# Preparation of keys, weights and angles moved into the attention loop of a two-layer cross-attention and expert kernel

## The reference, cut to what matters

```python
x = x + _L0_xattn_ref(_layernorm(x), ctx_2048, Wq, Wk, Wv, Wo, q_norm_w, k_norm_w, pos_BxS2, itok)   # 16 heads, 4 key heads of 128
x = x + _L0_ffn_ref(_layernorm(x), ...)                  # 32 experts, top 6, and shared ones
x = x + _L1_xattn_ref(_layernorm(x), ctx_2048, seg_id, W_kvc, W_dq, W_uq, W_qr, W_uk, W_kr, W_uv, W_o)
x = x + _L1_ffn_ref(_layernorm(x), ...)
...
kv_in = jnp.concatenate([context_hidden, draft_hidden], axis=1)          # 1601 + 256 = 1857 rows
k = _rms_norm((kv_in @ Wk.T).reshape(bsz, total_len, KVH, HD), k_norm_w)
q = _rope(q, draft_position_ids); k = _rope(k, full_position_ids)
probs = jax.nn.softmax(jnp.einsum('bhqd,bhkd->bhqk', q, k) * SCALE, axis=-1)
...
kv_c = kv @ W_kvc                                        # third block
k_rope = _rope(kv_c @ W_kr, lk)
```

## Time and profile before

| | |
|---|---|
| median of 3 runs | 1956.87 us |
| the profiled execution, first to last instruction | 1959.5 us |
| PE, DVE, ACT, POOL busy | 88%, 74%, 55%, 56% |
| `prepare` (first DMA to the first load of `attend`) | 0.72 to 128.60 us |
| first score matmul of group 0 | 173.94 us |
| one group in the steady part | 72.8 us |

### The profile page before, as it was taken

How to read it: one execution, slowest core, us unless ns; L and a number is a source line. 1 busy time by engine, 2 the same in 40 slices (tenths; PEclk the granted TensorE clock), 3 DMA queues, 4 the chain that set the end, 5 groups by cost and what they waited for, 6 DMA issues and landing times. The chain is left out here.

```text
span 1959.5 us, 41434 instructions
## 1 busy us (share of the span) xinstructions
PE 1725.4 (88%) x14663; PEld 1326.9 (68%) x14663; DVE 1442.7 (74%) x3812; ACT 1070.1 (55%) x2650; POOL 1091.2 (56%) x1657
## 2 busy tenths in 40 slices
PE   3346999999999999999999999996899999079997
PEld 3234787787787778778778778775555555038974
DVE  7838878877877877877877887875757775675746
ACT  3324766767666667666666766763133333073543
POOL 4525866866866776776776776710156664072210
PEclk9678999999999999999999999997899999595998
DMA  7683021121021022022022020144369996510100
GB/s 283 227 323 130 2 89 46 45 88 57 34 88 69 22 89 75 16 89 88 2 89 88 2 89 13 49 147 184 109 198 272 270 269 194 163 31 16 44 10 26
DMA packets 76663, 201.96 MB, mean 103 GB/s; under 512 B 9993, under 2 KB 42866, under 8 KB 73266
## 3 DMA queue, kind: packets, MB, share of 16 engines
q1 hardware_dynamic: 63314, 163.70, 24.5%
q0 software_dynamic: 9984, 30.42, 4.6%
q10 hardware_dynamic: 3168, 5.24, 0.7%
HBM read 161.67 MB, written 37.66 MB: 102 GB/s over the span
## 5 line engine op out<-in xcount | busy, mean ns | idle before, releaser
L893 DVE TENSOR_TENSOR att_pT<-att_pT 128x512 bf16<-128x512 f32 (+1 forms) x512 | 321.2, 651 | 179.7 <-ACT att_pT L790 176.5
L643 PE MATMUL att_out<-att_V,att_pT 128*128 128x128 bf16 x5760 | 386.0, 220 | 10.0 <-DVE att_pT L893 8.3
L643 PEld LDWEIGHTS att_out<-att_V,att_pT 128*128 128x128 bf16 x5760 | 349.6, 98 | 37.5 <-DVE att_pT L893 19.7
L790 ACT ACTIVATE att_pT<-att_pT 128x512 bf16<-128x512 f32 (+1 forms) x512 | 277.9, 572 | 175.6 <-PE att_pT L631 175.6
L796 ACT ACTIVATE att_prob<-att_scores,att_negmax 128x512 f32<-128x512 f32 (+1 forms) x512 | 329.8, 654 | 21.1 <-DVE att_negmax L882 18.9
L622 PE MATMUL att_scores<-att_K,att_Q 128*128 128x512 bf16 (+1 forms) x1536 | 324.1, 361 | 1.0 <-DVE att_K L855 1.0
L880 DVE TENSOR_REDUCE att_mx<-att_scores 128x1 f32<-128x512 f32 (+1 forms) x512 | 291.4, 631 | 1.2 <-PE att_scores L622 1.2
L631 PE MATMUL att_pT<-att_ident,att_prob 128*128 128x128 f32 x1920 | 274.3, 274 | 0.0
L622 PEld LDWEIGHTS att_scores<-att_K,att_Q 128*128 128x128 bf16 x1536 | 150.6, 98 | 145.4 <-issue 2.5
L582 PE MATMUL att_aux<-att_wkv,att_kvT 128*128 128x256 bf16 x1440 | 179.6, 274 | 43.8 <-DMA att_kvT<-kv_s 20.0
L631 PEld LDWEIGHTS att_pT<-att_ident,att_prob 128*128 128x128 f32 x1920 | 208.6, 141 | 0.9
(11 more groups left out here) (312 smaller groups left out, 3233.5 us busy)
## 6 DMA issues: line engine op xcount, KB each, us to landing
moe_wa<-in_wa_l SPq DMA_DIRECT2D x80, 480.0 KB
att_kvT<-kv_s SPq DMA_DIRECT2D x15, 1920.0 KB
att_tab<-tab_s SPq DMA_DIRECT2D x16, 960.0 KB, 11.5
att_wq<-wq_s SPq DMA_DIRECT2D x16, 512.0 KB
att_wo<-wo_s SPq DMA_DIRECT2D x16, 512.0 KB
kv_s<-prep_kvhl SPq DMA_DIRECT2D x4, 1920.0 KB
prep_kv<-in_ctx_l SPq DMA_DIRECT2D x4, 1664.0 KB, 8.1
moe_y<-y_s SPq DMA_DIRECT2D x8, 768.0 KB, 4.7
```

The source lines that it names most:

```text
L643: last = nc.tensor.matmul(out_ps[:, i % 2, :], pT[:, i % 2, a, k, :], V[:, par, k, w, :], start=(k, a, w) == (0, 0, 0), stop=(k, a) == (KT ...
L790: nc.scalar.activation(pT[:, i % 2, 0, 4 * j:4 * j + m, :], pT_ps[j % 2][:, 0:m, :], ACT.Copy).then_inc(s["pt_hi"], 1)
L893: nc.vector.tensor_tensor(pT[:, i % 2, 1, 4 * j:4 * j + m, :], pT_ps[j % 2][:, 0:m, :], pT[:, i % 2, 0, 4 * j:4 * j + m, :], ALU.subtract) ...
```

## The change

`prepare` is gone, with its scope. Its work goes into `attend`:

- Batch 0 is split in SBUF at the start: ACT makes the high halves of keys and weights, POOL the low halves of the keys, DVE those of the weights, and DVE forms the angles of batch 0 only. Nothing of it passes through DRAM before it is used. The first projections begin with context keys (KV2), not with the tokens.
- Batches 1 to 3 are split a quarter of the keys at a time: in groups 0 to 11, at the end of slot 2, ACT (`keys_high`) and then DVE (`keys_low`, with a sum of the keys).
- The remaining weights come in nine pieces in groups 0 to 2, high halves on ACT in slots 1 and 4, low halves on POOL (`weight_low`) after the third and the eighth rope of its sequence.
- The angles of the next batch are nine DVE steps, one a slot, in groups 1, 5, 9 and 2, 6, 10; the two Sin instructions stand on ACT at the end of slot 6 of groups 2, 6 and 10.
- The key table is made by quarters: a `TB` task on PE in slot 3 of every group (in bfloat16 halves now), a copy by ACT, the turning by POOL (`turn_rows`) after the sixth rope. A `MN` task gives the mean from the key sums. An `XT` task turns the next batch's tokens in groups 1, 5 and 9.
- POOL gathers batch by batch, in groups 4, 8 and 12, and for the last batch at the end.
- The halves of the keys stay in SBUF for a batch; the weights are written to DRAM and loaded again from group 4 on.

Core of the diff:

```diff
 SLOTS = [
     ([], [("KV", 0)], [("KV", 1)]),
     ([("AT-", 1)], [("KV", 2)], [("WO-", 1)]),
-    ([], [("Q", 0)], [("KV", 3)]),
-    ([], [("Q", 1)], [("KV", 4)]),
+    ([("XT", 0)], [("Q", 0)], [("KV", 3)]),
+    ([("TB", 0)], [("Q", 1)], [("KV", 4)]),
...
-    ([("KT", 2)], [("KT", 3)], []),
+    ([("KT", 2)], [("KT", 3)], [("MN", 0)]),
...
+PIECES_AT = {(0, 1): [(1, "O")], (0, 4): [(2, "K"), (2, "Q")], (1, 1): [(3, "K"), (3, "Q")], (1, 4): [(2, "O")], (2, 4): [(3, "O")]}
...
+                    elif kind == "TB":
+                        b, k = divmod(n, NB)
+                        pe.wait_ge(s["wcat_lo"], 1)
+                        keys_split(pe, min(k + 2, NB), b)
+                        for m in range(min(4, CT - 4 * k)):
+                            k0 = S + (4 * k + m) * P
+                            for c in range(DC):
+                                for a, w in ((0, 0), (0, 1), (1, 0)):
...
+                    if i == 2 and g < SPLITS:
+                        keys_high(g)
+                    for h, kind in PIECES_AT.get((g, i), ()):
+                        weight_high(h, kind)
+                    if i == 6 and g % KVH == 2 and g < (B - 1) * KVH:
+                        turn_table(g // KVH + 1)
...
+                def keys_low(g):
...
+                    nc.vector.tensor_tensor(kvT[:, b % 2, 1, :, cols], keys, kvT[:, b % 2, 0, :, cols], ALU.subtract).then_inc(s["c_lo"], 1)
+                    nc.vector.reduce_sum(sums[:, b, k, :], keys, AX.X).then_inc(s["c_sum"], 1)
...
+                def between(i, g):
+                    b = g // KVH + 1
+                    if (g, i) == (0, 0):
+                        for k in range(NB):
+                            nc.vector.reduce_sum(sums[:, 0, k, :], first_part(k), AX.X).then_inc(s["first_sum"], 1)
+                        weight_low_first("O")
...
+                    if g < SPLITS:
+                        if i == 2:
+                            keys_low(g)
+                        if g % KVH == 1 and i == 0:
+                            normal_rows(b)
+                        if g % KVH == 1 and i >= 3:
+                            angle(b, i - 3)
+                        if g % KVH == 2 and 1 <= i <= 4:
+                            angle(b, i + 4)
...
+                def turn_rows(n):
...
+                    nc.gpsimd.tensor_tensor(turned[:, 0, 0:m, :], keys, turns[:, 0, 0:m, :], ALU.mult).then_inc(s["turned"], 1)
+                    nc.gpsimd.tensor_tensor(turned[:, 1, 0:m, 0:RH], keys[:, :, RH:R1], turns[:, 1, 0:m, 0:RH], ALU.mult).then_inc(s["turned"], 1)
+                    nc.gpsimd.tensor_tensor(turned[:, 1, 0:m, RH:R1], keys[:, :, 0:RH], turns[:, 1, 0:m, RH:R1], ALU.mult).then_inc(s["turned"], 1)
...
+                    nc.gpsimd.tensor_tensor(keys, turned[:, 0, 0:m, :], turned[:, 1, 0:m, :], ALU.add).then_inc(s["tb_ready"], 1)
...
                 def prep(g, par):
-                    pool.wait_ge(tab_load[par], 16 * (g // 2 + 1))
+                    pool.wait_ge(s["trig_ready"], 2 * (g // KVH) + 2)
+                    now = g - 1
                     for order, (kind, n) in enumerate(POOL_ORDER):
                         rope(pool, order, kind, n, g, par)
+                        if order == 2:
+                            for h, k in PIECES_AT.get((now, 1), ()):
+                                weight_low(h, k)
+                        if order == 5:
+                            turn_rows(now)
+                            if now == 0:
+                                rstd(slice(2, TT), 2)
+                        if order == 7:
+                            for h, k in PIECES_AT.get((now, 4), ()):
+                                weight_low(h, k)
+                        if now >= KVH and now % KVH == 0:
+                            b = now // KVH - 1
+                            if order in (2, 6):
+                                gather(2 * b + order // 6)
+                            if order in (4, 8):
+                                store(2 * b + order // 8)
```

More of the change, by code:

```diff
@@ L488, in nth, with first_key_rows @@
+        FREE = {"KV": "kvraw_ready", "Q": "qraw_ready", "KT": "kt_lo", "QT": "qt_lo", "AT": "at_lo", "WO": "x_added", "XT": "xt_lo", "TB": "tb_raw", "MN": "mean_ready"}
         def nth(kind, n, g):
+            if kind in ("XT", "TB", "MN"):
+                return n + 1
+            if kind == "KV" and g == 0:
+                return FIRST_KV.index(n) + 1
             return PER_GROUP[kind] * g + n + 1
+        def first_key_rows(eng, pairs):
+            done = [p for p in FIRST_KV if p in pairs or FIRST_KV.index(p) < max(FIRST_KV.index(q) for q in pairs)]
+            wait(eng, s["kp_vector"], sum(("KV", p) not in FIRST_ON_POOL for p in done))
+            wait(eng, s["kp_pool"], sum(("KV", p) in FIRST_ON_POOL for p in done))
@@ L496, in key_rows @@
             elif g == 0:
-                on_pool = sum(("KV", j) in FIRST_ON_POOL for j in range(n + 1))
-                wait(eng, s["kp_vector"], n + 1 - on_pool)
-                wait(eng, s["kp_pool"], on_pool)
+                first_key_rows(eng, [2 * (n // 2), n])
         def bank_of(kind, n, g):
@@ L565, in task @@
                     par = (u + ahead) % 2
+                    b = gt // KVH
                     bank = bank_of(kind, n, gt)
-                    if gt or kind not in ("KT", "QT"):
+                    if not (gt == 0 and kind in ("KT", "QT")) and (kind, n) != ("XT", 0):
                         if before:
@@ L648, in slot @@
                 def slot(i, g, u, first, prep, last):
-                    ahead, amid, behind = (tasks_of(place, prep, first, last) for place in SLOTS[i])
+                    ahead, amid, behind = (tasks_of(place, prep, first, last, g) for place in SLOTS[i])
                     old = not (first and i == 0) and not (last and i > 0)
```

827 lines of the change are left out of this document (456 added, 371 removed).

## The result

Four runs of the changed kernel have a median of 1946.72 us (1944.51 to 1948.19), four of the kernel before, on the same chip, 1957.4 us (1956.04 to 1962.97). The ratio is 0.9939, with a 95% interval of 0.9924 to 0.9954. So the kernel is faster, by 11 us where 57 were forecast, and its time lies above the range of 1880 to 1920 us and above the wider one of 1864 to 1932.

What follows compares the result with a forecast made beforehand. PE, 98% busy, was taken to bound the kernel, with POOL's chain 0.8 us from the bound; 1959.5 - 114.9 (start) + 54.0 (groups) + 1.6 (DVE, group 0) + 3 (clock) = 1903.2 profiled, 1900 us median, range 1880 to 1920, wider 1864 to 1932.

Steps and rivals of the forecast that it cites:

- the 114.9 us: Start: first scores come near 59 us instead of 173.9, giving back 114.9 us.
- the first scores at 24 + 34.9: Start: rope chain begins at 24 us and takes 34.9 as before, so first scores at 59.
- 54.0 forecast: Attention groups: added POOL work costs 54.0 us in all, paid by PE as a wait of KT3 for POOL.
- POOL's chain in a group has 0.8 us to spare, against PE's none: Steady group: POOL ends KV7's rope only 0.8 us before PE's KT3 needs it.
- after 625.26 only one wait of 2.52 us is left on the way to KV7: Steady group: POOL's one later wait, 2.52 us, takes up added work standing before it; later work lengthens the group.
- `keys_low` with its sum is 2.2 in slot 2; DVE waits 2.34 there, so nothing: Slot 2, DVE: the added 2.2 us fit into its 2.34 us wait and cost nothing.
- so I charge nothing: Slot 6, ACT: 4.3 us for Sin, three times, covered by PE's slot 7 wait for POOL; without cover 6 us.
- PE alone (1869): Rival for the groups: PE alone sets the pace, its added tasks costing 25.4 us, plus 1.6; 1869 us, chance 0.17.
- Rival 2: Groups: waits lower the clock in most groups, not three, 22 to 33 us on top; 1920 to 1935 us, chance 0.17.
- The forecast's own 3 us for the clock: Groups 0 to 2: POOL's stalls lower PE's clock, costing 3 us in all.
- Rival 3: Start: first stage not short, first scores at 80 to 90 us; kernel 1921 to 1931 us, chance 0.07.
- Rival 4: All 16 groups: POOL late through every rope; slower if each grows over 7.2 us, 2000 us with 10; chance 0.04.

Runs made afterwards that it cites:

- the experiment on the start: Changed kernel, POOL's first rope not waiting for the small product, second head's low weight halves held until DVE's last rope: 1941.65 us, ratio 0.9911.
- the placed version: Changed kernel with the start's two edits, rows behind last rope, keys rounded in slot 1, angles, Sin, deviations, mean, gathers and weights re-placed: 1894.0 us, ratio 0.9661.
- the last version: The placed version with Sin in slot 0 of groups 3, 7, 11, POOL's weight pieces re-placed, `first_rows` moved to group 3: 1878.83 us, ratio 0.9586.

## Why the prediction was wrong

**The start** was right in kind: of the 114.9 us that it was to give back, 108.05 came (173.94 to 65.89). The chain began at 25.18 (24 forecast). What failed is "the first scores at 24 + 34.9": the chain itself was 5.8 us longer than in the kernel before, and the experiment on the start returned 5.2 of them (its chain took 35.3, from 25.39 to 60.72). One part, POOL's wait for the small product, was foreseen but held in the 4 us ahead of the chain; it came inside. The other, turns taken by DVE and POOL, was charged in the angles and not in the chain's last steps, beside the second head's weights. The Trainium skill (SBUF — State Buffer, "SBUF: two separate sides") describes the port pair that these two share as an exclusive lock: a DVE instruction with two inputs in SBUF waits out the whole of a GpSimd instruction that reads SBUF and began first. By that rule DVE's step of 0.22 us ends just behind POOL's, and the trace agrees (63.24 and 63.17 us). One reading of the earlier trace rows was loose, without harm: DVE's step there ended 2.0 us after POOL's and not just after it, which is about the step's own length (2.16), so the conclusion that the two took turns stands.

**The groups** hold the large miss: 54.0 forecast and 95.1 measured. The step that failed is "POOL's chain in a group has 0.8 us to spare, against PE's none", and what was built on it: that POOL's lateness at KT3 is the whole price and all else lies beside it. KT3 waited 16.7 us for POOL in all the groups, not 54; the rest of the 95.1 was paid by PE's own added tasks and by its waits for DVE and ACT in other slots. Three readings under it were wrong.

- "after 625.26 only one wait of 2.52 us is left on the way to KV7": that wait is not spare time ahead of a fixed end. What ends it is DVE's sum in slot 3, which moves with every delay of slots 2 and 3. So the chain starts anew there, and PE's added task of 1.50 us is paid ahead of POOL's rows, not beside them. Rows 5 of the kernel before had the releaser's name; it should have been followed to the task ahead of it. The wait went from 2.52 to 3.84, and back to 2.51 with the task moved. The forecast took POOL's price in place of PE's 25.4 us; in group 13, where nothing else was added, the two came to 2.6 together (1.7 forecast).
- "`keys_low` with its sum is 2.2 in slot 2; DVE waits 2.34 there, so nothing": the new instruction brought a wait of its own, for ACT, and the 2.34 us were gone before it began. Rounding the keys one slot earlier returned 15 us, the largest of the terms put at nothing.
- "so I charge nothing" for Sin, and POOL's lateness as the cover for the angles: the slots became late first, and a POOL fed by late slots is not late again. PE waits for POOL 1.39 us in group 2 (5.4 forecast) and none in group 5 (4.8). The angles cost some 6 to 8 us. Sin's own share was measured only in the placed version: 3.3 a group and more at a bad place, 1.9 at a good one.

What POOL itself cost was sized fairly well in the groups without angles: 1.10 against 1.7 in group 13, 3.46 against 3.8 in group 8; moving the rows returned 20.3 us. POOL was busy 75% of groups 0 to 2 where 85% were forecast.

Of the rivals, PE alone (1869) is what the last version comes near to: 32.9 us in the groups against its 25.4 + 1.6. Rival 2 came true in two groups only: the lower clock cost groups 4 and 12 3.7 us together, and the granted clock of all other groups is 1.00, but for group 0 (0.98). The forecast's own 3 us for the clock fits this in size by luck, as it was meant for groups 0 to 2. Rival 3's first scores at 80 to 90 did not come. Rival 4's 7.2 us a group came close to being paid on average (95.1 / 16 = 5.9), but not by its mechanism: PE's waits were for DVE, POOL and ACT in turn, beside its own added tasks.

## What to carry to other kernels

An idle time is room only up to what ends it: follow the releaser, and if it moves with the work that is added, the wait moves along and the prices add. A piece put into an idle stretch must have its inputs at the stretch's beginning; one slot earlier on the engine that feeds it was worth 15 us here. And a cover by another engine's lateness is to be charged in full until a trace shows it, since engines fed by the same slots are late together.

## Unexpected on the hardware

- The mean's task, 16 matmuls of one row by 64 columns in float32, takes PE 1.05 us and costs a group 1.1 to 1.3 us with the turn of its bank, in both slots where it stood; 0.5 was forecast. The trace of the kernel before had the price: 26 matmuls of this shape in 1.61 us (line 221).
- The same DVE subtraction of 768 columns took 1.73 us behind its wait and 0.95 us with the rounding one slot earlier. What POOL did beside it is the difference:

```profile
336.77 1.27 POOL L644 TENSOR_TENSOR att_scaled<-att_qraw,att_qw 128x512 f32<-128x512 f32 x1
```

DVE's step began at 337.12, 0.92 us before this one ended, and 0.81 us of its 1.73 are left behind that. In the other run POOL's step beside it ended after 0.14 us, and 0.81 us are left again. They take turns, as in the start.

- The table load took 1.28 us in each of the shown places, with Sin right behind it in group 2 (297.55 + 1.28 = 298.83, and Sin at 298.85).
